# Graph layer on Trainium2: edge sums as one fp32 matmul per tile instead of two single-pass matmuls on a high and a low part

## The reference

```
xn = _layernorm(x)
m = jnp.concatenate([h[edge_src], w], axis=1)          # h = xn
tmp = jax.nn.relu(m @ W1.T + b1)                       # one message of 256 per edge
h_N = jax.ops.segment_sum(tmp, edge_dst, num_segments=h.shape[0])
h_lin = jax.nn.relu(jnp.concatenate([h, h_N], axis=1) @ W2.T)      # then divided by its norm
x = x + gnn(xn) + mix(xn)          # mix: 4 layers of linear attention and a GELU feed-forward
x = x + ffn(_layernorm(x))         # 16 experts, the best 2 of each node, then a layernorm
```

## Time and profile before

| | |
|---|---|
| median of 3 runs | 2796.87 us |
| profiled execution | 2794.38 us |
| its span, first to last instruction | 2792.6 us |
| mean granted TensorE clock | 0.906 of full |
| PE matmul busy | 2204.5 us (79%) |
| DVE busy | 1592.0 us (57%) |
| POOL busy | 1337.1 us (48%) |
| ACT busy | 1063.5 us (38%) |

### The profile page before, as it was taken

How to read it: one execution, slowest core, us unless ns; L and a number is a source line. 1 busy time by engine, 2 the same in 40 slices (tenths; PEclk the granted TensorE clock), 3 DMA queues, 4 the chain that set the end, 5 groups by cost and what they waited for, 6 DMA issues and landing times. The chain is left out here.

```text
span 2792.6 us, 43955 instructions
## 1 busy us (share of the span) xinstructions
PE 2204.5 (79%) x10622; PEld 1790.6 (64%) x10622; DVE 1592.0 (57%) x3709; ACT 1063.5 (38%) x2363; POOL 1337.1 (48%) x1224
## 2 busy tenths in 40 slices
PE   1348888897888889888988988888897747999940
PEld 1236666676666667666766766666675637999940
DVE  3647766666766666676666667766664561000016
ACT  1235444444444444444444445444442322222210
POOL 3145555565555556655555665655565002221135
PEclk9769999999989999998999999899997868999975
DMA  5522222224222222422222242222223116888843
GB/s 163 163 78 57 68 61 61 61 66 103 58 65 60 61 60 67 105 58 65 61 60 61 68 106 55 62 60 58 60 68 85 65 46 227 251 255 253 254 122 100
DMA packets 257568, 269.38 MB, mean 96 GB/s; under 512 B 145195, under 2 KB 198082, under 8 KB 257406
## 3 DMA queue, kind: packets, MB, share of 16 engines
q0 software_dynamic: 124672, 132.82, 20.1%
q1 hardware_dynamic: 132734, 134.91, 15.1%
HBM read 238.22 MB, written 28.37 MB: 95 GB/s over the span
## 5 line engine op out<-in xcount | busy, mean ns | idle before, releaser
L423 POOL DMA_INDIRECT G<-P_d,stage x896 | 1146.6, 1280 | 861.5 <-DVE z L402 572.2
L370 ACT ACTIVATE zr<-z 125x512 fp32r<-125x512 f32 x448 | 274.9, 638 | 517.1 <-DVE z L402 517.0
L402 DVE TENSOR_TENSOR z<-bank,G 125x512 f32<-125x512 f32 x448 | 292.4, 686 | 298.5 <-PE bank L362 194.5
L1147 PE MATMUL bank<-TT,W_s 128*128 128x250 f32 (+1 forms) x1280 | 381.3, 450 | 5.0 <-ACT TT L801 4.1
L1018 PE MATMUL bank<-W_s,hid 128*125 128x256 f32 x1600 | 359.6, 379 | 0.0
L1147 PEld LDWEIGHTS bank<-TT,W_s 128*128 128x128 f32 x1280 | 248.2, 200 | 112.6 <-issue 17.0
L1018 PEld LDWEIGHTS bank<-W_s,hid 128*125 128x125 f32 x1600 | 292.6, 187 | 42.8
L376 DVE SCALAR_TENSOR_TENSOR zl<-z,zr 125x512 fp32r<-125x512 f32 x448 | 288.1, 684 | 38.4 <-ACT zr L370 37.1
L354 PE MATMUL bank<-zr,onehot 125*125 125x256 f32 x896 | 269.0, 332 | 11.2 <-DVE zl L376 11.2
L1012 PE MATMUL bank<-ident,hn 125*128 125x125 f32 x700 | 140.8, 311 | 166.9 <-DVE hn L1359 77.6
L801 ACT ACTIVATE TT<-bank,lnc 128x125 f32<-128x125 f32 x600 | 214.4, 476 | 42.7 <-PE bank L1012 42.7
(11 more groups left out here) (284 smaller groups left out, 3368.5 us busy)
## 6 DMA issues: line engine op xcount, KB each, us to landing
W_s<-in_L_ffn_w SPq DMA_DIRECT2D x64, 512.0 KB, 4.5
hid<-in_L_ffn_w SPq DMA_DIRECT2D x64, 512.0 KB, 4.6
G<-P_d,stage POOLq DMA_INDIRECT x896, 4.2
W_s<-in_L_mix_W SPq DMA_DIRECT2D x8, 1024.0 KB
aT<-attr_d SPq DMA_DIRECT2D x224, 31.2 KB
b2e<-in_L_ffn_b SPq DMA_DIRECT2D x32, 128.0 KB, 5.4
eT<-in_L_ffn_b SPq DMA_DIRECT2D x32, 128.0 KB, 5.5
slot_out<-yo SPq DMA_DIRECT2D x32, 128.0 KB, 2.1
```

What stands on the lines that cost most here:

```text
L370: nc.scalar.activation(zr[:, s, k, :], z[:, k, :], ACT.Relu).then_inc(r_done, 1)
L402: nc.vector.tensor_tensor(z[:, k, :], edge_bank[k][0:ET, :], G[:, ST * s + 2 * k:ST * s + 2 * k + 2, :].rearrange("p j d -> p (j d)"), ALU ...
L423: nc.gpsimd.indirect_dma_start(G[:, j, :], None, P_d[:, :], bass.IndirectOffsetOnAxis(ap=stage[s][:, j:j + 1], axis=0)).then_inc(g_in[j], 16)
L1147: ins = pe.matmul(to[:, 0:(b - a) * T], W1_s[:, k, part], TT[:, k, TT_PIECES[pc]], start=k == 0, stop=k == KD - 1)
```

## The change

`zr` and `onehot` become plain float32 tensors. `zl`, `dve_low` and the semaphore `lo_done` go. Each subtile has one fp32 matmul on `zr`. PE waits for ACT's `r_done` where it waited for DVE's `lo_done`. DVE waits, ahead of each half of `z` that it overwrites, until ACT has read that half in the step before.

```
@@ buffers
-        zr = sb("zr", [ET, PG, 2, 2 * D], f32r)
-        zl = sb("zl", [ET, 2, 2 * D], f32r)
-        onehot = sb("onehot", [ET, PG, ST, T], f32r)
+        zr = sb("zr", [ET, PG, 2, 2 * D])
+        onehot = sb("onehot", [ET, PG, ST, T])
@@ pe_sums
                 if i % 2 == 0:
-                    nc.tensor.wait_ge(lo_done, ge * 2 + (i // 2 + 3))
-                nc.tensor.matmul(sum_bank[0:T, 0:D], onehot[:, s, i, :], zr[:, s, i // 2, cols], start=i == 0, stop=False)
-                ins = nc.tensor.matmul(sum_bank[0:T, 0:D], onehot[:, s, i, :], zl[:, i // 2, cols], start=False, stop=i == ST - 1)
+                    nc.tensor.wait_ge(r_done, ge * 2 + (i // 2 + 1))
+                ins = nc.tensor.matmul(sum_bank[0:T, 0:D], onehot[:, s, i, :], zr[:, s, i // 2, cols], start=i == 0, stop=i == ST - 1)
@@ dve_low
-        def dve_low(ge, s):
-
-            for k in range(2):
-                nc.vector.wait_ge(r_done, ge * 2 + (k + 1))
-                nc.vector.scalar_tensor_tensor(zl[:, k, :], z[:, k, :], 0.0, zr[:, s, k, :].bitcast(f32), ALU.max, ALU.subtract).then_inc(lo_done, 1)
-
@@ dve_edges
-            nc.vector.wait_ge(lo_done, ge * 2 + 2)
             for k in range(2):
+                if not first:
+                    nc.vector.wait_ge(r_done, ge * 2 + (k - 1))
                 nc.vector.wait_ge(e_done, ge * 2 + (k + 1))
...
             if not first:
                 dve_acc(ge - 1, reg)
-            dve_low(ge, s)
             if not last:
                 dve_onehot(e + 1, ge + 1, 1 - s)
```

More of the change, by code:

```diff
@@ L284, in build @@
         a_out = [sem(f"a_out{i}") for i in range(AB)]
-        st_ready, e_done, z_done, r_done, lo_done, oh_done, s_done, acc_done = (sem(n) for n in (
-            "st_ready", "e_done", "z_done", "r_done", "lo_done", "oh_done", "s_done", "acc_done"))
+        st_ready, e_done, z_done, r_done, oh_done, s_done, acc_done = (sem(n) for n in (
+            "st_ready", "e_done", "z_done", "r_done", "oh_done", "s_done", "acc_done"))
         g_in = [sem(f"g_in{i}") for i in range(PG * ST)]
@@ L1265, in _ @@
             dve.sem_inc(acc_done, 1)
-            dve.sem_inc(lo_done, 2)
             dve.sem_inc(row_dve, 1)
```

## The result

| | before | after |
|---|---|---|
| time, median of 4 runs (us) | 2796.72 (2794.96 to 2797.74) | 2832.57 (2819.57 to 2835.81) |
| profiled execution (its span) | 2794.4 (2792.6) | 2834.86 (2833.1) |

The ratio is 1.012, with a 95% interval of 1.0087 to 1.0153. The same kernel measured once more, on another chip where the kernel before took 2793.33 us, gave 2821.35 us (1.0099, 1.0072 to 1.0125), 28 us more.

What follows compares the result with a forecast made beforehand. PE was taken to carry the second pass, with PE and DVE leaning on each other in the first. Second pass +89, first pass +4, openings 0, middles -5 give +88 us: forecast 2885 us, 3.1% slower, range 2848 to 2915.

Steps and rivals of the forecast that it cites:

- the gap of 3.65 us at a group's start: Second-pass group start, PE waiting for DVE's residual: follows PE's own last product and stays, 3.65 us.
- the relief: DVE loses 288 us of busy time by the removed instructions, hidden behind PE nearly everywhere.
- 5 for `zl`: Last second-pass group of a layer: PE's waits for `zl`, 6.0 us, go; -5 us.
- 0.77 in 20 first-pass groups: Second step of a first-pass group: 0.77 us more PE time, taken up as the `V5` wait shrinks.
- The price of a matmul: Edge steps on PE: fp32 matmul 0.43 us, float32r 0.12 us, so each step gains 0.77 us.
- the `hn` wait: Second pass, behind step 0: wait falls from 1.9 to 1.1 us, hiding 0.77 us in 20 groups, -15 us.
- First pass: First-pass groups stay at 20.1 us; +0.2 for each of 20 groups, +4 us, bounds -14 and +15.
- the `V5` wait: First-pass group, behind the second step: PE's wait for the copy shrinks from 1.75 to about 1.0 us.
- Middles: PE's wait for DVE's queries, 4.15 us, gets 1.28 us shorter once in each of 4 layers; -5 us.
- Second-pass groups: Groups last 76 to 77 us instead of 71.8; 160 steps, +123 us gross, +89 us after what hides it.
- rival 2: Gathers pace the second pass, hiding 0.77 us in 80 steps: -62 us, about 2823 us; chance 7%.
- Rival 3: An fp32 matmul costs as much as two float32r ones, PE's work unchanged: about 2769 us; chance 4%.

Runs made afterwards that it cites:

- 2: Kernel before with the change on TensorE alone (one fp32 product per tile, VectorE still computes `zl`): 2879.22 us (1.0298).
- 5: Kernel after with idle increments where VectorE's removed instructions stood, so its loops stand where they did in the kernel before: 2837.92 us (1.0162).
- 7: Kernel after: 16 idle increments at VectorE's end 2792.2 us; 128 there 2790.45; 16 ahead of layer loop 2780.03; unchanged 2821.35; last, 16 at TensorE's end 2791.18.
- 1: Kernel after with two idle increments ahead of each of the eight edge steps in VectorE's second-pass loop: 2783.6 us (0.9943).
- 4: Kernel after with 16 idle increments ahead of VectorE's second-pass loop: 2771.89 us (0.9907); repeated on another chip 2767.41 us (0.9890).
- 6: Kernel before: 33 idle increments ahead of VectorE's second-pass loop 2734.2 us; that loop written out 2723.53 us; all three VectorE layer loops written out 2686.06 us.
- 8: VectorE's three loops written out: kernel after 2752.72 us (0.9856); kernel before with the change on TensorE alone 2757.37 us (0.9854).

## Why the prediction was wrong

Three kernels lie on the way from before to after. In medians:

| step | us | difference |
|---|---|---|
| before | 2796.7 | |
| change on TensorE alone (2) | 2879.2 | +82.6 |
| VectorE's low part removed, its loops where they were (5) | 2837.9 | -41.3 |
| VectorE's loops at the places of the kernel after (16 increments at the end, 7) | 2792.2 | -45.7 |
| the kernel after: 20 late starts instead of 8 | 2832.6 | +40.4 |

The kernels with 2837.9 and 2792.2 us ran on the same chip and have 8 late starts each, so their difference is the cleanest of the table. The first of them also runs two idle increments in each step; how much that costs is bounded by 1 and 4, on one chip and without late starts, where the kernel with increments in its loop is 12 us slower than that with as many ahead of it. The other differences are between chips.

**The step that failed** is the line on the gap of 3.65 us at a group's start, which "follows PE's own last product and stays". It follows VectorE's jump back, and it went. The row was read correctly as a wait for VectorE's residual, but not asked why VectorE was late: VectorE had been idle "by issue" for 4.22 us ahead of it, and the straight-line groups had no such gap; both were in the trace. The forecast's sum has no term for it. It is worth 62 us in the kernel before (6) and 34 to 46 in the kernel after, where VectorE has more slack.

**What was not in it at all** is the late starts, about +40 us, which no row of the kernel before could show. They come from late increments of PE, and the chip may have a part in them (7). The two misses point in opposite ways and nearly cancel, which is luck; the third makes the difference: 88 - 46 - 46 + 40 = 36 us.

**The rest of the sum was too high.** With the loops where they were the change costs +41.8 us (5, against the kernel before on its chip), not +88. Two parts:
- PE's part alone: my terms without what the relief was to give (5 for `zl`, 5 in the middles, 0.77 in 20 first-pass groups, 15) make about 88 + 25 = 113 us; measured 82.6, and 64 to 71 without jumps. The price of a matmul was right to 0.01 us and the `hn` wait took what it should. The 16 second-pass intervals grew by 4.25 us each (1135.7 to 1203.7 us), where the terms make 94/20 = 4.7, and the 16 first-pass intervals by 6.6 us together (326.7 to 333.3), where 16 x 0.77 is 12.3. So in the first pass about half of what I had counted in full is hidden; by what was not followed.
- The relief: some 25 us in my terms, 41.3 measured (2 to 5). It was not sized too small by itself, since written-out kernels give 18 to 25 (8). The 12 second-pass intervals with a jump got 27.3 us shorter (920.2 to 892.9 us) and the four without none (283.5 and 284.3): with less to do, VectorE's idle time at a jump is 3.0 to 3.4 us instead of 4.1 to 4.4, and PE waits 32.4 us for the residual instead of 44.2. Most of the difference is the gap once more.

**First pass:** 20.1 us were forecast, 20.3 come when VectorE is not late (1, 4 and 7): +0.2 a group, which is what the sum had, and the `V5` wait is the forecast 1.0 us (15.7 us in 15 waits in the last kernel of 7). The 20.8 to 23.8 us of the kernel after are the late starts.

**Middles:** the queries wait fell from 4.15 to at most 1.5 us, more than the 1.28 expected.

**Second-pass groups:** 76 to 77 us were expected with the gap in them. Between the kernel before with its loop moved and the kernel after with 16 increments ahead of it, neither with a gap, the mean interval goes from 66.4 to 70.3 us: +3.9 where the sum had +4.45. So this term was nearly right, and hidden in the result by the gap that went.

**The rivals:** the time came nearest to rival 2 (2823 us), but not by its mechanism: PE's steps 1 to 4 did get longer (6.37 us apart instead of 5.58), and no wait for gathers took their place. Rival 3 is refuted by the row of 1.72 us.

## What to carry to other kernels

When an engine is idle "by issue" at the head of a loop, count the packets of its instruction queue in that window and compare with a straight copy of the body: an edit that only moves a loop can give or take more than the edit itself. Measure a change at more than one layout (idle increments ahead of the loop, or the loops written out in both kernels), with both kernels of a comparison on the same chip, before giving the difference to its arithmetic; here the same change reads +28 or +36 us as it stands, +42 with the loops where they were and +67 with them written out. When an engine seems late on data that are there, look at when the other engine's increment is recorded. Where memory for code allows it, write out the loops of the engine that is late: that alone gave 107 us here, against the 36 us of the change.

## What the runs showed of the hardware that I had not expected

- **The refill hangs on place, not on length.** VectorE's loops written from 1043 to 1588 fetch their program again in every turn (18 packets in four groups, in three kernels). Loops from 1012 to 1541, 1012 to 1557, 1019 to 1548, 1028 to 1557 and 1076 to 1621 don't (3 packets, in five kernels). The second and the last of these are as long as the first, 545 instructions. That a store of a fixed number of 8 KB blocks lies behind it, of which the first loop touches one more, fits all eight kernels and foretold the gap's return in 5 and its going in 6; the store and its size were not measured.
- **The idle time of a refill** is 3.0 to 3.4 us in the kernel of 5 and 4.2 to 5.4 us in the kernel before, for VectorE; it costs PE up to 4.8 us, and then a stretch at the lower clock.
- **What the lower clock costs a group.** In the kernel after, groups of 70.2 and 71.5 us differ in one row, the product behind the `hn` transposes, at full and at half speed (the granted clock is 1.00 from 829.90 to 833.00 us and 0.61 from 900.07 to 904.00):

```profile
829.90 2.48 PE L1139 MATMUL bank<-TT,W_s 128*128 128x375 f32 x8 [0.35 <-ACT TT L793]
...
900.07 3.86 PE L1139 MATMUL bank<-TT,W_s 128*128 128x375 f32 x8 [0.35 <-ACT TT L793]
```

- **PE's semaphore increment can come 0.7 to 2.3 us behind the modelled end of its matmul**, in steps of 0.75 us, half the distance of POOL's gathers: in every first-pass group of one kernel on two chips, in 8 or 9 of 20 in four others, and never in five runs on two further chips, nor in the kernel before. Its cause stays open (7).
